# A block of state-space scan, attention and gated network: convolution, squares and low parts change engines, and all orders are new

## The reference

```
x = x + layernorm(attn(layernorm(x)));  x = x + layernorm(ffn(layernorm(x)))

attn:  n = rms_norm(xm);  value, gate = n @ in_proj_w                 # 256 channels each
       value = silu(conv(value, 4 taps, per channel, causal) + conv_b)
       Bm, Cm = xm @ B_proj_w, xm @ C_proj_w                          # 16 heads x 64
       y = selective_scan(value, A, Bm, Cm, dt) + D * value
       xm = xm + scale * ((y * silu(gate)) @ out_proj_w)
       xm = xm + scale * (relu(rms_norm(xm) @ m_fc_w) ** 2 @ m_proj_w)     # first MLP
       q, k, v = rms_norm(xa) @ q_w, k_w, v_w;  q, k normed and rotated    # 16 and 4 heads x 8
       xa = xa + scale * (softmax(causal(q k^T)) v @ o_w)
       xa = xa + scale * (relu(rms_norm(xa) @ a_fc_w) ** 2 @ a_proj_w)     # second MLP
ffn:   h = silu(x @ w1) * (x @ w2)                                    # 512 wide, ternary weights
       h = gelu(h @ h1);  h = gelu(h @ h2);  out = h @ w3
```

## Time and profile before

| | us |
|---|---|
| three timed runs: median (lowest to highest) | 976.28 (975.53 to 977.0) |
| the profiled execution: its own time | 976.42 |
| its span | 974.7 |
| TensorE busy | 888.5 (91%) |
| VectorE busy | 667.8 (69%) |
| ScalarE busy | 578.2 (59%) |
| GpSimd busy | 460.0 (47%) |

### The profile page before, as it was taken

One profiled execution on the slowest core, in us unless ns is written; L12 is line 12 of the kernel. 1 busy time (PEld: TensorE's weight loads), 2 busy tenths in 40 slices (PEclk: granted clock), 3 DMA queues, 4 the chain that ended last, 5 costly groups with the idle time before them and its releaser, 6 DMA issues.

```text
span 974.7 us, 24913 instructions
## 1 busy us (share of the span) xinstructions
PE 888.5 (91%) x9248; PEld 758.0 (78%) x9248; DVE 667.8 (69%) x1803; ACT 578.2 (59%) x1220; POOL 460.0 (47%) x708
## 2 busy tenths in 40 slices
PE   0689989999999999998999999999999999989785
PEld 0667768787979888987878898888877887878575
DVE  5978969866777767758576884875776686746320
ACT  3644365766747557746565768567475575575532
POOL 1574344625543637435345545355263644463432
PEclk9999999999999999999999999999999999999899
DMA  8100000000000000000000000000000000000000
GB/s 280 59 17 7 7 7 2 7 1 13 7 13 7 13 2 7 13 12 6 12 7 2 17 2 12 8 12 7 12 2 2 2 13 1 13 1 13 12 3 9
DMA packets 17926, 15.71 MB, mean 16 GB/s; under 512 B 2064, under 2 KB 15760, under 8 KB 17552
## 3 DMA queue, kind: packets, MB, share of 16 engines
q1 hardware_dynamic: 17808, 14.12, 4.6%
HBM read 12.02 MB, written 2.10 MB: 14 GB/s over the span
## 4 chain that ended last, share of the span: by engine, by line
PE 64%; DVE 22%; issue 7%; ACT 3%; POOL 2%; DMA 1%; SPq 0%; POOLq 0%; DVEq 0%; ACTq 0%
PE pool L1170 59%; PE pool L1187 5%; DVE mneg L1064 2%; DVE val L951 2%; DVE M L961 1%; DVE M L962 1%; ACT PT L726 1%; DVE W L1018 1%; DVE val L949 1%; DVE gAB L1144 1%; DVE W L1020 1%; POOL PT L496 1%; DMA X<-in_x 1%; DVE LM L852 1%; DVE val L968 1%
## 5 line engine op out<-in xcount | busy, mean ns | idle before, releaser
L1064 DVE TENSOR_REDUCE mneg<-pool 128x2 f32<-128x512 f32 (+1 forms) x192 | 119.0, 683 | 54.7 <-PE pool L1170 54.7
L1170 PE MATMUL pool<-gH,w_h_hi 128*128 128x256 f32 x512 | 149.1, 291 | 4.8 <-POOL gL L542 2.2
L1170 PE MATMUL pool<-gL,w_h_hi 128*128 128x256 f32 x512 | 143.8, 281 | 0.0
L1170 PE MATMUL pool<-gH,w_h_lo 128*128 128x256 f32 x512 | 143.8, 281 | 0.0
L961 DVE TENSOR_TENSOR M<-pool,LM 128x512 f32<-128x512 f32 x128 | 87.6, 685 | 55.2 <-PE pool L1170 54.8
L726 ACT ACTIVATE PT<-pool 128x512 f32<-128x512 f32 x192 | 99.2, 603 | 31.8 <-PE pool L1170 31.5
L1170 PE MATMUL pool<-BC 64*128 64x256 f32 (+1 forms) x1024 | 111.4, 345 | 3.3 <-ACT PT L726 1.7
L496 POOL TENSOR_SCALAR_AFFINE_SELECT PT<-PT 128x256 f32<-128x256 f32 (+1 forms) x192 | 89.2, 488 | 42.4 <-ACT PT L726 39.0
L1170 PEld LDWEIGHTS pool<-BC 64*128 64x128 f32 x1024 | 87.6, 187 | 26.1 <-issue 14.1
L644 ACT ACTIVATE BC<-pool 128x512 f32<-128x512 f32 x128 | 75.6, 603 | 54.2 <-PE pool L1170 50.9
L1170 PEld LDWEIGHTS pool<-gH,w_h_hi 128*128 128x128 f32 x512 | 96.9, 189 | 7.2 <-issue 3.2
(11 more groups left out here) (235 smaller groups left out, 2428.0 us busy)
## 6 DMA issues: line engine op xcount, KB each, us to landing
X<-in_x SPq DMA_DIRECT2D x16, 128.0 KB, 2.1
x<-in_x SPq DMA_DIRECT2D x16, 128.0 KB, 2.2
out<-ob SPq DMA_DIRECT2D x16, 128.0 KB, 2.1
hid<-in_w_h SPq DMA_DIRECT2D x1, 1024.0 KB, 8.9
gAB<-in_w_h SPq DMA_DIRECT2D x1, 1024.0 KB, 9.4
PT<-in_w_B SPq DMA_DIRECT2D x1, 512.0 KB, 4.9
PT<-in_w_C SPq DMA_DIRECT2D x1, 512.0 KB, 6.4
Qs<-in_s SPq DMA_DIRECT2D x1, 512.0 KB, 5.0
```

Of the source, the lines that this page charges most:

```text
L1064: v.reduce_max(dst, o, axis=AX.X, negate=True).then_inc(S["mx"], 1)
L1170: return p.matmul(o, lhsT, rhs, start=start, stop=True, skip_group_check=True)
```

## The change

VectorE's convolution reads the bank of inv itself, tap by tap with the newest first: tap k adds the first 256 - k columns into val from column k on, so no zero columns are needed; va and vpad go. The bank is free when the last conv has run. The squares of both MLPs move from GpSimd to VectorE as max(bank, 0) times the relu in hid, so up's and upb's banks are held until then. glo and hlo move from GpSimd to VectorE unchanged. X gets a third buffer, and loadx of batch i waits for tin of i - 3. Among the first loads, rows moves ahead and a third loadx follows the second. The orders of all engines and the banks are new. GpSimd's xr gets a wait for its own earlier part.

```diff
 PER = dict(...)            # va=1 taken out
 BANKS_OF = dict(
-    tin=(1, "xnlo"), inv=(1, "va"), gat=(1, "ga"), ...
-    ... up=(1, "relu"), ... upb=(1, "relub"),
+    tin=(1, "xnlo"), inv=(1, "conv"), gat=(1, "ga"), ...
+    ... up=(1, "sq"), ... upb=(1, "sqb"),
 ORDERS = dict(             # all of them new; each starts so:
   PE
-        "tin inv gat bc bc bc cb cb cb bc bc bc vt v cb cb bc v cb cb bc v cb tin v inv bc gat bc cb cb out bc bc bc vt t2 cb "
+        "tin bc bc bc inv cb bc bc bc bc cb cb gat bc cb vt cb tin v v cb cb cb v bc bc inv v bc bc bc cb cb cb gat out bc bc "
...
-        "downb h2 h2 w3 t6 w1 w1 w2 w2 h1 h1 h2 h2 w3"
+        "upb h2 downb h2 w3 t6 w1 w1 w2 w2 h1 h1 h2 h2 w3"
   Activation
-        "pxx phi phi ss1 phi pex pex pex pex pex pex pex pex xnhi va ga bcx bcx bcx ss1 bcx bcx val fhi bcx xp fhi fhi fhi "
+        "pxx phi ss1 phi phi pex pex pex pex pex pex pex xnhi bcx pex bcx bcx bcx bcx bcx ss1 ga val xp bcx bcx xnhi fhi fhi "
   DVE
-        "st0 dec ag0 st0 ag0 xh m01 dec xh dec plo dec xm dec plo dec nrm plo plm plm plm plm plm plm plm plm xnlo fold fold "
+        "st0 dec ag0 xh dec dec m01 xm dec dec st0 nrm plo ag0 dec plo plm plm plm plo fold st0 xnlo fold plm plm plm plm xh "
   SP
-        "loadx loadx loady loady loadx loadx loadx loadx loady store loadx loady store loadx loady store loadx loady store "
+        "loadx loadx loady loady loadx loadx loadx loadx store store loady loadx loady loadx loady store loadx loadx loady "
 BANKS = (...)              # new
-    S_x = [sem("x_in0"), sem("x_in1")]
+    S_x = [sem("x_in0"), sem("x_in1"), sem("x_in2")]
-    X, xh, xm = sb("X", [P, 2, T, D]), ...
-    vpad = sb("vpad", [P, 2, L + KC - 1])
+    X, xh, xm = sb("X", [P, 3, T, D]), ...
 # SyncE
         def loadx(i, _):
-            if i >= 2:
-                sp.wait_ge(S["tin"], at("tin", i - 2))
-            sp.dma_start(X[:, i % 2], ...).then_inc(S_x[i % 2], 16)
+            if i >= 3:
+                sp.wait_ge(S["tin"], at("tin", i - 3))
+            sp.dma_start(X[:, i % 3], ...).then_inc(S_x[i % 3], 16)
         loadx(0, 0)
         sp.dma_start(heads[:], t["heads"]).then_inc(in_h, 16)
+        sp.dma_start(rows[:], t["rows"]).then_inc(in_h, 16)
-        for dst, src in ((rows[:], "rows"), (cols[:], "cols"), (raw_in, "w_in"), (ident[:], "c_ident")):
+        for dst, src in ((ident[:], "c_ident"), (raw_in, "w_in"), (cols[:], "cols")):
...
         loadx(1, 0)
+        loadx(2, 0)
 # GpSimd: sq, sqb_, glo and hlo are taken out; the memset of vpad too
 # ScalarE
-        def va(i, _):
-            act.wait_ge(S["inv"], at("inv", i))
...
-            a.activation(vpad[:, :, KC - 1:], halves(bank("inv", i)), ACT.Copy).then_inc(S["va"], 1)
 # VectorE
         def conv(i, k):
             if k == 0:
-                dve.wait_ge(S["va"], at("va", i))
+                dve.wait_ge(S["inv"], at("inv", i))
...
             for b in range(2):
-                w, dst = cols[:, C_CW + b * KC + k:C_CW + b * KC + k + 1], val[:, i % 2, b, :]
+                c = C_CW + b * KC + KC - 1 - k
+                src, dst = halves(bank("inv", i))[:, b, 0:L - k], val[:, i % 2, b, k:]
                 if k == 0:
-                    last = v.tensor_scalar(dst, vpad[:, b, 0:L], w, cols[:, C_CB + b:C_CB + b + 1], ALU.mult, ALU.add)
+                    last = v.tensor_scalar(dst, src, cols[:, c:c + 1], cols[:, C_CB + b:C_CB + b + 1], ALU.mult, ALU.add)
                 else:
-                    last = v.scalar_tensor_tensor(dst, vpad[:, b, k:k + L], w, dst, ALU.mult, ALU.add)
+                    last = v.scalar_tensor_tensor(dst, src, cols[:, c:c + 1], dst, ALU.mult, ALU.add)
+        def sq(i, k):                                  # sqb_ is the same on hid[:, 1] and upb
+            dve.wait_ge(S["relu"], at("relu", i, k))
+            h = hid[:, 0, 2 * k:2 * k + 2, :]
+            v.scalar_tensor_tensor(h, halves(bank("up", i, k)), 0.0, h, ALU.max, ALU.mult).then_inc(S["sq"], 1)
+        def glo(i, k):                                 # hlo is the same on gB, after hhi
+            dve.wait_ge(S["ghi"], at("ghi", i, k))
+            J = slice(2 * k, 2 * k + 2)
+            v.tensor_tensor(gL[:, J], gA[:, J], gH[:, J].bitcast(F32), ALU.subtract).then_inc(S["glo"], 1)
```

More of the change, by code:

```diff
@@ L40 @@
 BANKS_OF = dict(
-    tin=(1, "xnlo"), inv=(1, "va"), gat=(1, "ga"), vt=(1, "xp"), bc=(1, "bcx"), cb=(2, "m"), v=(1, "yg"), out=(1, "xm2"),
-    t2=(1, "t2c"), up=(1, "relu"), down=(1, "xa"), t3=(1, "t3c"), qkv=(1, "rp"), qt=(1, "qtc"), kt=(1, "ktc"), s=(4, "mx"),
-    mt=(1, "qm"), e=(4, "ex"), pv=(1, "yv"), yt=(1, "yn"), t4=(1, "t4c"), o=(1, "xa2"), t5=(1, "t5c"), upb=(1, "relub"),
+    tin=(1, "xnlo"), inv=(1, "conv"), gat=(1, "ga"), vt=(1, "xp"), bc=(1, "bcx"), cb=(2, "m"), v=(1, "yg"), out=(1, "xm2"),
+    t2=(1, "t2c"), up=(1, "sq"), down=(1, "xa"), t3=(1, "t3c"), qkv=(1, "rp"), qt=(1, "qtc"), kt=(1, "ktc"), s=(4, "mx"),
+    mt=(1, "qm"), e=(4, "ex"), pv=(1, "yv"), yt=(1, "yn"), t4=(1, "t4c"), o=(1, "xa2"), t5=(1, "t5c"), upb=(1, "sqb"),
     downb=(1, "xa3"), t6=(1, "t6lo"), w1=(1, "sl"), w2=(1, "gt"), h1=(1, "ge1"), h2=(1, "ge2"), w3=(1, "ln3"))
@@ new lines @@
+        "ge1 ktc bcx bcx bcx qtc qtc val hhi ge1 xp ss4 bcx bcx ga t2c ss2 bcx bcx ss1 ex ex ex relub relub hhi ex relu bcx "
+        "ex ex relu ex ex ex ex ex ex ge2 ss3 ge2 t6hi yv sl t3c sl t4c ghi xnhi ghi qk ss4 vv ge1 ge1 hhi ss2 bcx t5c bcx "
+        "hhi t2c bcx val ga bcx bcx bcx ss1 ktc qtc xp relu qtc bcx bcx relu ge2 xnhi ge2 ex ex ex ex relub relub ex ex ex "
[4 rows of a table added]
+        "ss2 vv bcx ge1 relu relu val hhi t5c ss1 bcx bcx ge1 bcx bcx hhi qtc ktc xp qtc bcx bcx bcx ge2 relub relub ge2 ex "
[4 rows of a table added]
@@ L172 @@
+        "r6 sel x1 sel r7 sel sel r7 sel sel sel sel r5 r8 r8 r5 outp r6 r6 x1 r7 r7 r8 r8 outp r8 r8 outp"
+    ),
+    SP=(
+        "loadx loadx loady loady loadx loadx loadx loadx store store loady loadx loady loadx loady store loadx loadx loady "
+        "store loady store loadx store loady loady store loadx loadx store loady loady store store loady store loady store "
+        "loady loady store store loady store store"
     ),
@@ L217, in _banks @@
             per = PER[giver]
-            last = 0 if name == "qkv" else per - 1 if name in HELD or name in ("yt", "mt") or per == 1 else k * count + j if count == 4 else k
+            last = 0 if name == "qkv" else per - 1 if name in HELD or name in ("inv", "yt", "mt") or per == 1 else k * count + j if count == 4 else k
             holder[b] = (giver, i, last)
@@ L385, in _ @@
             sp.dma_start(dst, t[src]).then_inc(in_e, 16)
-        run("SP", dict(loadx=lambda n, _: loadx(n + 2, _), loady=loady, store=store))
+        run("SP", dict(loadx=lambda n, _: loadx(n + 3, _), loady=loady, store=store))
         sp.wait_ge(S_out, 16 * BATCH)
@@ L806, in ge2 @@
             a.activation(gA[:, 2 * k:2 * k + 2, :], halves(bank("h2", i, k)), ACT.Gelu).then_inc(S["ge2"], 1)
-        run("Activation", dict(pxx=pxx, pex=pex, phi=phi, fhi=fhi, ss1=ss1, xnhi=xnhi, va=va, ga=ga, val=val_, xp=xp, bcx=bcx, ss2=ss2, t2c=t2c,
+        run("Activation", dict(pxx=pxx, pex=pex, phi=phi, fhi=fhi, ss1=ss1, xnhi=xnhi, ga=ga, val=val_, xp=xp, bcx=bcx, ss2=ss2, t2c=t2c,
                                relu=relu, ss3=ss3, t3c=t3c, qk=qk, vv=vv, qtc=qtc, ktc=ktc, ex=ex, yv=yv_, t4c=t4c,
@@ L908, in st0 @@
         def st0(i, _):
-            dve.wait_ge(S_x[i % 2], 16 * (i // 2 + 1))
-            stats(0, i, "st0", X[:, i % 2], "ag0")
+            dve.wait_ge(S_x[i % 3], 16 * (i // 3 + 1))
+            stats(0, i, "st0", X[:, i % 3], "ag0")
         def ag0(i, _):
@@ L987, in xa_, with sqb_ @@
             last.then_inc(S["xa"], 1)
+        def sq(i, k):
+            dve.wait_ge(S["relu"], at("relu", i, k))
+            h = hid[:, 0, 2 * k:2 * k + 2, :]
+            v.scalar_tensor_tensor(h, halves(bank("up", i, k)), 0.0, h, ALU.max, ALU.mult).then_inc(S["sq"], 1)
+        def sqb_(i, k):
+            dve.wait_ge(S["relub"], at("relub", i, k))
+            h = hid[:, 1, 2 * k:2 * k + 2, :]
+            v.scalar_tensor_tensor(h, halves(bank("upb", i, k)), 0.0, h, ALU.max, ALU.mult).then_inc(S["sqb"], 1)
         def e2(i, _):
@@ L1144, in gt, with hlo @@
             v.tensor_tensor(x, halves(bank("w2", i, k)), x, ALU.mult).then_inc(S["gt"], 1)
+        def glo(i, k):
+            dve.wait_ge(S["ghi"], at("ghi", i, k))
+            J = slice(2 * k, 2 * k + 2)
+            v.tensor_tensor(gL[:, J], gA[:, J], gH[:, J].bitcast(F32), ALU.subtract).then_inc(S["glo"], 1)
+        def hlo(i, k):
+            dve.wait_ge(S["hhi"], at("hhi", i, k))
+            J = slice(2 * k, 2 * k + 2)
+            v.tensor_tensor(gL[:, J], gB[:, J], gH[:, J].bitcast(F32), ALU.subtract).then_inc(S["hlo"], 1)
         def st3(i, _):
@@ L1198, in tin @@
             if i == 0:
-                pe.wait_ge(in_a, 16 * 4)
+                pe.wait_ge(in_a, 16 * 3)
```

(2 more changed lines are left out.)

101 lines of the change are left out of this document (34 added, 67 removed), and 181 rows, old and new, of tables (Activation, DVE, PE, Pool).

## The result

The changed kernel takes 933.75 us (median of four runs, 932.34 to 935.34). Beside it, on the same chip, the kernel before took 975.9. The ratio is 0.9567 [0.9549, 0.9585]: 42 us faster, where 10 were forecast, and outside the range of 952 to 985. The profiled execution took 935.34 us, its span is 933.6, and the mean granted clock of TensorE is 0.996 (0.988 before).

What follows compares the result with a forecast made beforehand. The prediction saw a full TensorE pipeline between a start waiting for VectorE and an end waiting for whole chains. Its sum was 976.3 - 6 (start) + 1 (middle) - 5 (end) = 966.3 us, range 952 to 985.

Steps and rivals of the forecast that it cites:

- the -5 for shorter chains and the new order: Middle: shorter va, low-part and square chains, and more TensorE work between dependent parts, were given 5 us of gain.
- Only its 86 us without work can be won: Whole kernel: as all TensorE work stays, only its 86 us of idle time was taken as winnable.
- The start, -6: Start: VectorE's new order lets TensorE's first matmuls that count begin 6 us sooner; bounds 0 and 7.
- The rival that it is given back: First 200 us: the start's 6 us and half of the end are lost, giving 975; chance 0.10.
- VectorE's load, 740: VectorE's busy time: squares and low parts added, convolution cheaper, forecast at 740 us, 72 more.
- The middle, +1: 150 to 850 us: load price of 6 less 5 for chains and order; bounds -15 and +25.
- a price for the load (+6): Middle: VectorE rising from 73% to 81% costs TensorE 6 us, at 0.9 us for 8 points.
- The bound of +25: Middle's upper bound: the whole 700 us lose at half the excess of 100 to 200.
- The end, -5: End: 2.3 us from the last chain and 3 from waits ahead of pv and w1; bounds -1 and -8.
- -2.3 on the chain that ended last: End: low parts and squares on the last chain take 3.5 us on VectorE instead of 5.8 on GpSimd.
- New order fills the middle: Rival, middle: 12 of the 17 us of TensorE idle go, giving 953; chance 0.15.
- VectorE becomes the bound: Rival, 150 to 850 us: denser VectorE stretches make TensorE lose up to 25 us, giving 990; chance 0.20.

Runs made afterwards that it cites:

- start_new: The kernel before with the new start alone: new orders up to the first xnlo and new order of first loads, two x buffers; 0.9991 of before, 977.74 us.
- va_back: The kernel after with ScalarE's copy to vpad and the convolution from vpad again; 0.9669 of before, 947.5 us.
- before_half: The kernel before, with GpSimd's squares and low parts cut to half of the columns from the second batch on; 0.9839 of before, 963.56 us.
- after_short: The kernel after, with VectorE's squares and low parts cut to 16 of 256 columns from the second batch on; 0.949 of before, 929.21 us.
- pool_net: The kernel after with the low parts glo and hlo alone on GpSimd again; 0.9689 of before, 946.45 us.
- pool_sq: The kernel after with the squares sq and sqb alone on GpSimd again; 0.9682 of before, 946.56 us.
- order_old_half: New orders with all work placed as before, GpSimd's squares and low parts cut to half of the columns from the second batch on; 0.9741 of before, 951.64 us.
- order_old_places: The kernel after's orders, banks, third x buffer and loads, with va, squares, low parts and convolution source as in the kernel before; 0.9936 of before, 973.23 us.
- sqnet_old_order: The kernel before with squares and low parts moved to VectorE, in the old orders, convolution from vpad; 1.0215 of before, 1000.66 us.
- after_net_twice: The kernel after with VectorE computing each of the 64 low parts twice, first to a spare tile; 0.9822 of before, 962.53 us.

## Why the prediction was wrong

By stage, 10 us were forecast as 6 + 0 - 1 + 5 (start, filling, middle, end); the runs gave 7.4 + 9.1 + 15.1 + 9.4. The step that failed most is the middle, and in it the -5 for shorter chains and the new order; the filling, put at nothing, comes next.

**"Only its 86 us without work can be won".** This step failed first, since it made the cases too narrow. Idle time fell by 30 us; another 11.1 went out of the busy time. Gaps shorter than a matmul are counted as busy, and so is work at the lower clock. The mean granted clock times the span gives 11.7 us of full speed lost before (0.012 x 974.7) and 3.7 after (0.004 x 933.6), so up to 8 of the 42 us; less, where TensorE was idle anyway. The earlier trace rows show it: 50 to 100 is at 0.93 before and 1.00 after. The 0.93 is a part of the time at 1.2 GHz instead of 2.4, in a stretch in which TensorE stood idle for 6.5 us; after, it is 1.00 in every stretch shown up to 850. So a gap could cost twice, and I had priced it once.

**The start, -6.** Right: 7.4 at the first matmul that counts, whose times were 22.33 and 29.72. The rival that it is given back was true of the old orders (start_new) and false of the new, which keep 5 us of it.

**The filling, 0.** This term was missing without a reason. I took the start as a stage and the middle from 150 on, and gave what lies between no term. It brought 9.1 us. 6.6 us of lateness in that stage hang on the convolution alone (va_back), whose step I costed by VectorE's busy time, and not by its chain: inv, a copy in ScalarE's queue, conv, val, vt, xp, v.

**VectorE's load, 740.** Over-sized: 713. The squares take 0.67 us and not 0.73, which is 4 us; the low parts are as estimated, and hardly held (688 and 693 ns against a median of 685 and 686); the convolution loses 14 instead of 11. (The "at best minus 18" had no sum: 0.41 us for each first tap makes it 13.) Kept apart, 668 + 86 - 14 would be 740, so 27 us went from other instructions, for which I had 10. before_half shows this by itself: VectorE's work is the same as before, only GpSimd's steps are halved, and VectorE's busy time falls by 18.7 us from the 667.8 of the earlier trace rows:

```profile
PE 886.7 (92%) x9248; PEld 756.8 (79%) x9248; DVE 649.1 (67%) x1803; ACT 577.3 (60%) x1220; POOL 402.9 (42%) x708
```

GpSimd at 304 and ScalarE at 570.5 came out as said (310 and 572).

The Trainium skill, "VectorE: DVE Perf Modes", Rules for kernel authors, would have the bank copied to SBUF first. Here the measurement decides against it: from PSUM the taps take 474 ns at the median, from SBUF they took 479 with a mean of 612, and with the copy put back the kernel is 10 us slower (va_back). The first tap, though, does cost more from PSUM: 536 ns at the median where it took 410. The prediction had 470 for it, and never looked at its median; as instructions from SBUF were held now and then, its mean was 564, and so the move did not lose there.

**The middle, +1.** This is the largest miss: -15.1, at the bound of -15 that I had given for the case that nearly all 17 us of idle go. It was the sum of a price for the load (+6) and shorter chains and the new order (-5), and the -5 is what failed. In the kernel after, cutting the four steps to 16 columns takes 58 us of VectorE's work away and brings 3.3 us in the middle, 7.5 in all (after_short). So the +6 was, if anything, too much, but of the right size. Against it, put back one at a time, the old convolution costs 5.3 us in the middle, the low parts on GpSimd 7.1 and the squares 8.6 (lateness of va_back, pool_net and pool_sq against that of the kernel after), and these 21 us are already net of the load. I had given 5 to all of them and to the order together.

The way to the +6 was luck, though. I read 0.9 us of TensorE for 8 points of VectorE from stretches of one kernel, and the runs show no such constant: the new orders take the steps nearly free (0.13 us for each), twice the low parts cost 0.57, where this slope gave 5 to 8 us for the 25 measured, and the same four steps are +21 us in the old orders and -26 in the new. I treated the orders as a thing beside the placement. How much of the 21 us is the shorter step and how much the shorter queue of GpSimd is open: at half of the columns a step of GpSimd is about as long as the whole one of VectorE, and order_old_half brings 19 of the 26 us that lie between order_old_places and va_back, but it shortens the queue as well. Up to 3.4 us of the 15.1 are clock (20 x 0.08 + 20 x 0.09). Two stretches of the kernel before, columns as in the earlier trace rows:

```profile
440.00:460.00 20.00, 16.86 (x153) 14.84 (x153) 19.35 (x50) 11.86 (x32) 11.90 (x16) 0.92 0.03 8
800.00:820.00 20.00, 18.07 (x198) 16.05 (x194) 14.74 (x35) 8.30 (x16) 8.85 (x14) 0.91 0.01 2
```

The new order also puts more of TensorE's work between a bc and its cb (7.5 us instead of 3.2, mean of the first ones of each batch), between e and pv (6.3 instead of 4.6, the same) and between the last h1 and the first h2 (7.8 instead of 4.9), counted at the lengths of the table; I had seen that and given it no number of its own. That it helps is argued and not shown: order_old_places has the same distances and loses 10 us in the middle.

The bound of +25 doesn't come out of its reason either: half of the excess of 100 to 200 is 2.65 us in 100, 18.6 in 700. It played no part in the miss. The chances for "faster" add up to 0.72, not 0.71.

**The end, -5.** It brought 9.4, and not by the term that I thought surest. The two waits of the earlier trace rows are gone; with what stands between them they are 8.2 us between 800 and 820 us of work (lateness grows by 9.1 before and by 0.9 after), where I had counted 3. Most of the end's gain is the orders' doing: order_old_places, with all work at its old place, has 7.3 us of it, and waits neither ahead of that pv nor ahead of that w1. The wait on the last square went too: behind upb of batch 15 the kernel before lost 2.4 us (GpSimd's 2.00 in the earlier trace rows), the one after nothing. Its order has an h2 of 3 us between upb and downb, and order_old_places, whose squares are still GpSimd's, doesn't wait there either. But from 820 us of work to the end the lateness grows by 13.2 us and not by 11.7: the first low part of batch 15 is shorter and comes no sooner, as the rows of 907 to 910 show, and the last 33 us are at a granted clock of 0.88, while the kernel before had its low stretch ahead of the last chain (0.86 in 900 to 925). So the term "-2.3 on the chain that ended last" isn't borne out: the low parts gave nothing there, and the squares' wait went by the order.

**The rivals.** "New order fills the middle" was the nearest, with 953, and too small by its own premise, because it capped the middle at the idle time. "VectorE becomes the bound" is true of the old orders (sqnet_old_order), and of the new ones only when the low parts are doubled (after_net_twice), not of the kernel after.

**Open.** Both transplants (order_old_places, sqnet_old_order) use orders that were not made for their placement. Whether orders made for the old placement would gain as much wasn't tried, so "the placement brings 26 us" holds for these orders alone. VectorE's load and the length of its steps always changed together, and so did the length of GpSimd's steps and its queue. The new banks were not tried without the new orders. The convolution from PSUM in the old orders, where the bank of inv would be held until the last tap, wasn't tried, nor two x buffers in the new ones. Which of the changed distances in the order brings most of the 24 us isn't told apart.

## What to carry to other kernels

When queues are fixed by hand, judge a move and its order together: the same move was worth +21 and -26 us. Count TensorE's losses as lateness against its own work, since busy time hides short gaps and low clock, and give the filling of the pipeline its own term. The free time of the engine that receives a step is no price for it, and neither is a slope read from one kernel: steps that the order was made for cost 0.13 us for each us, in the two other cases tried it was 0.56 and 0.57.

## What the runs showed of the hardware that was not expected

- VectorE is slowed by GpSimd's work more than the convolution shows: halving 120 of GpSimd's tensor_tensor steps (460.0 to 402.9 us) took 18.7 us off VectorE's unchanged work, and only 4.7 of them off the convolution (71.6 to 66.9; before_half).
- A scalar_tensor_tensor of 128x512 with one input from PSUM takes 680 to 683 ns, the same as a tensor_tensor of that size (683 to 686); so two operations in one instruction cost nothing extra here.
- For the convolution the source matters in the first tap and not in the others. The first tap, a tensor_scalar of 256 columns with two scalars from SBUF, takes 410 ns at the median from SBUF and 536 from PSUM, 126 more; the scalar_tensor_tensor taps take 479 and 474. The long ones, up to 1377 and 1515 ns, are only among those from SBUF. The first tap before and after, columns as in the earlier trace rows:

```profile
L949 DVE TENSOR_SCALAR val<-vpad,cols x32: 400/410/1377, 32.1 to 779.6; 128x256 f32<-128x256 f32 x32
L925 DVE TENSOR_SCALAR val<-pool,cols x32: 528/536/550, 27.8 to 746.9; 128x256 f32<-128x256 f32 x32
```
